# VectorE's drains replaced by a semaphore of its own, in a two-layer graph kernel on one core

## The chip, the cores and the metric

The kernel runs on one core of a Trainium2 chip. The metric is the time that the device needs for one execution, in microseconds. Before the change it is 2659.04 us, the median of three runs (2654.21 to 2662.23). The engines are TensorE (PE in the profile; PEld is its weight load), VectorE (DVE), ScalarE (ACT), GpSimd (POOL) and SyncE (SP). A "q" behind the name (DVEq, SPq) is that engine's own queue of instructions that occupy no datapath, such as a drain or the issue of a DMA.

## The reference, cut to what matters

Two layers over one graph of 8192 nodes with 128 features each. `adj` is an 8192x8192 matrix of zeros and ones in float32 (256 MB), thin except in its first rows.

```python
# layer 0: attention over the neighbours
h = relu(layernorm(x));  H = h @ W.T + b;  s = H @ a_s;  r = H @ a_r
e = leaky_relu(A * s + A * r.T);  att = softmax(where(A > 0, e, NEG), axis=1)
x = x + att @ H
# layer 1: sum over the neighbours, then the maximum over them
h = relu(layernorm(x)) @ weight
out = relu(adj @ h + bias)
x = x + max over the neighbours j of row i of out[j]
```

## The kernel before

A tile is 128 rows of the graph, and there are 64. Tile 0, with the densest rows (the hubs), is handled by separate code. The work has these stages.

**Stream (about 0 to 1150 us).** `load_tile(n)` on SP brings 4 MB of `adj` into one of two buffers. It waits until PE has packed tile n-2. PE's `pack(n)` (L1037) folds eight columns into one word, and `number_words(n)` (L1046) adds the word's number; it writes to one of two halves of PSUM. VectorE's `extract(n)` (L1358 to L1402) then turns the 1024 words of each row into a list of neighbours: it takes the eight largest (MAX8), strikes them out (MATCH_REPLACE8, which the profile shows as a MATCH_VALUE_LOAD and the replacement), and so on; it unpacks the bits and repeats the game over the found nodes. Each of these operations reads what the one before wrote, and a `dve.drain()` stands between every two. Tiles come in four groups, and the denser tiles (1 to 11, steps 16 to 26) take more rounds.

**Ranking and attention (about 230 to 1400 us, inside the stream).** When the last tile of a group is extracted, `classify` and `rank_rows` on VectorE sort its rows by degree. POOL scatters the records (L670) once the rank is there (L1456), and from then on handles ranked tiles q: `gather_h` (L684) fetches one row of H per neighbour slot and partition with an indirect DMA into a ring of 64 slots. ScalarE forms raw scores (L833, L834), VectorE's `scores(q)` (L1468, L1470) makes their maximum, ScalarE exponentiates (L842) and scales the gathered rows (L850), PE sums them (L1093, L1094), VectorE's `close(q)` (L1492, L1494) divides, ScalarE normalizes, PE multiplies with the second weight, and POOL scatters the row into `y_table` (L694). In which step n of the stream each q has its turn stands in a written table (`STEP`); every engine runs its program strictly in that order, so a wait of one q holds back the tiles behind it on the same engine.

**Dense rows of layer 1 (about 1400 to 1800 us).** VectorE unpacks bits (L1567) and PE multiplies them (L1210). POOL gathers the rows of the thin tiles (L717), and VectorE adds them up in `sum_rows` (L1485, L1625 to L1630).

**Maximum over the neighbours (1800 us to the end).** POOL gathers rows of `p_table` for 66 tiles in turn (L758). It may be four tiles ahead of VectorE's `best_of(n)` (L1485, L1715) and waits for room in the ring. `best_of` reduces a tile's slots with max; before it, `hot_tile(n)` (L1764) builds one-hot columns with which PE turns the rows back into their order (L1231). Between the tiles up to n = 35 VectorE also picks the neighbours of the hub rows out of `adj`: 60 times `hub_round` (L1668, L1671) and 48 times `hub_pick` (L1678, L1681). `hub_work` spreads them in proportion to POOL's slots.

**Order on VectorE.** A wait that a program states before an operation rides on that operation; where two are stated, the first becomes a small instruction of its own. A `then_inc` rides on the operation, or on a drain where it is written on the drain. In the kernel before nearly every signal that VectorE gives to another engine is written on a drain.

Of the kernel before, what the change touches and what calls it, by code (L numbers as in the profile page):

```python
# [9 lines left out]
P = 128  # L10
N = 8192
D = 128
T = N // P
# [222 lines left out]
def build(nc, x, adj, W0, b0, a_s, a_r, W1, b1, out):  # L236
    ctx = ExitStack()
    with ctx:
# [6 lines left out]
        def sem(name):  # L245
# [202 lines left out]
        s_unpacked, s_bits, s_bitsfree, s_relu, s_ptr, s_prow = (  # L448
            sem(n) for n in ("s_unpacked", "s_bits", "s_bitsfree", "s_relu", "s_ptr", "s_prow"))
# [25 lines left out]
        def _(sp):  # L475
# [84 lines left out]
            for c in range(DENSE_BATCHES):  # L560
                if c + 2 < DENSE_BATCHES:
                    sp.wait_ge(s_unpacked, c + 1)
# [705 lines left out]
        def _(dve):  # L1268
            dve.memset(eps_col[:], EPS)
# [61 lines left out]
            def statistics(n):  # L1331
                for j in range(8):
                    dve.bn_stats(stats[:, j, :], xs[:, 8 * n + j, :])
                dve.drain()
                for j in range(8):
                    dve.bn_aggr(mv[:, 8 * n + j, :], stats[:, j, :])
                dve.drain().then_inc(s_var, 1)

            def shifts(n):
                cols = slice(8 * n, 8 * n + 8)  # L1340
                dve.wait_ge(s_scale, n + 1)
                dve.scalar_tensor_tensor(shift[:, cols], mv[:, cols, 0], -1.0, rstd[:, cols], ALU.mult, ALU.mult)
                dve.drain().then_inc(s_rstd, 1)
# [14 lines left out]
            def extract(n):  # L1358
# [18 lines left out]
                dve.tensor_scalar(words_i[:, 0:taken], words[:, 0:taken], VSCALE, None, ALU.mult)  # L1377
                dve.drain()
# [3 lines left out]
                                  bit_mask[:].unsqueeze(1).to_broadcast(wide), ALU.bitwise_and)  # L1382
                dve.drain()
                dve.tensor_tensor(node[:, 0:taken, :], words_no[:, 0:taken].unsqueeze(2).to_broadcast(wide),
                                  bit_node[:].unsqueeze(1).to_broadcast(wide), ALU.add)
                dve.drain()
                flat = node[:, 0:taken, :].rearrange("p a b -> p (a b)")
                dve.scalar_tensor_tensor(flat, bits[:, 0:taken, :].rearrange("p a b -> p (a b)"), 0.0, flat,
                                         ALU.is_gt, ALU.mult, accum_out=with_own[:, t:t + 1])
                dve.drain()  # L1390
                dve.scalar_tensor_tensor(flat, flat, label[:, t:t + 1], flat, ALU.not_equal, ALU.mult,
                                         accum_out=without[:, t:t + 1])
                dve.drain()
                dve.max(found[:, 0:8], flat)
                dve.drain()
                for r in range(8, w, 8):
                    dve.match_replace(flat, found[:, r - 8:r], flat, 0.0)
                    dve.drain()
                    dve.max(found[:, r:r + 8], flat)
                    dve.drain()  # L1400
# [3 lines left out]
            def classify(g):  # L1404
# [6 lines left out]
                dve.tensor_scalar(held, rec[g][:, :, lists], 0.0, None, ALU.is_gt)  # L1411
                dve.drain()
                dve.tensor_reduce(degree[:, cols], held, AX.X, ALU.add)
                dve.tensor_copy(rec_u[g][:, :, lists], rec[g][:, :, lists])
                dve.drain()
                dve.tensor_scalar(row_class[:, 0:n], degree[:, cols], float(m - 1), None, ALU.min)
                dve.tensor_tensor(own[:, cols], with_own[:, cols], without[:, cols], ALU.subtract)
                dve.drain()
                dve.tensor_tensor(one_hot[:, 0:m * n].rearrange("p (c t) -> p c t", t=n),
                                  row_class[:, 0:n].unsqueeze(1).to_broadcast([P, m, n]),  # L1420
                                  class_no[:, max(CLASSES) - m:max(CLASSES)].unsqueeze(2).to_broadcast([P, m, n]), ALU.is_equal)
                dve.drain().then_inc(s_onehot, 1)
# [425 lines left out]
```

## Time and profile before

| | us |
|---|---|
| median of three runs | 2659.04 |
| lowest and highest | 2654.21, 2662.23 |
| profiled execution, its own time | 2658.55 |
| span of its records | 2656.8 |
| PE busy | 1292.3 (49%) |
| DVE busy | 1519.5 (57%) |
| ACT busy | 465.0 (18%) |
| POOL busy | 1422.1 (54%) |

Busy time counts operations on the datapath; a drain is not in it. An engine's idle time is split by what ended it. "Issue" is time in which the engine waited for nothing that the profile shows, neither a semaphore nor an operation before it. "Remote" and "another core or an unknown queue" are waits whose releaser the records do not name. The granted clock of TensorE was 0.725 of full speed on average.

### The profile page before, as it was taken

The page shows a single profiled execution, that of the slowest core. Times are in us where ns is not written, and L with a number is a line of the kernel's source. Part 1 is how long each engine was busy: PE and PEld are TensorE (multiplying, and loading weights), DVE is VectorE, ACT ScalarE, POOL GpSimd, SP SyncE. Part 2 cuts the span into 40 slices and gives each one's busy share as a digit, 9 for nine tenths or more (in the row PEclk, how much of TensorE's full clock was granted, in tenths as well). Part 3 has the DMA queues.
Part 4 walks back from the last instruction along what each step waited for, and adds up shares of the span by engine and source line. Part 5 has one row for each costly group of instructions (what it writes and reads, how often), then busy time and mean ns, then how long its engine had stood idle before and what let it go on. Part 6 is the DMA issues. An engine that isn't in the chain of part 4 may idle for free.

```text
span 2656.8 us, 20293 instructions
## 1 busy us (share of the span) xinstructions
PE 1292.3 (49%) x5093; PEld 670.8 (25%) x5093; DVE 1519.5 (57%) x3498; ACT 465.0 (18%) x1561; POOL 1422.1 (54%) x1465
## 2 busy tenths in 40 slices
PE   3765145636153645533445997862442212475036
PEld 1432023313032312323441443320111100132013
DVE  6888757866442625436244654454658755893234
ACT  1541134502122402443450000000000000000000
POOL 0002655461746463567535556366757775567763
PEclk8887668777676866765676998885676555687568
DMA  9999857787773879852343223114112321212221
GB/s 343 398 372 410 266 164 281 283 278 295 265 288 107 329 249 380 343 180 66 81 132 81 71 63 80 30 48 89 51 45 67 91 75 36 53 50 52 71 69 44
DMA packets 161767, 443.50 MB, mean 167 GB/s; under 512 B 31986, under 2 KB 90661, under 8 KB 128750
## 3 DMA queue, kind: packets, MB, share of 16 engines
q1 hardware_dynamic: 78974, 307.90, 30.4%
q0 software_dynamic: 49360, 108.63, 15.9%
q10 hardware_dynamic: 33312, 25.63, 3.2%
q8 instruction: 43, 0.70, 0.1%
q14 instruction: 78, 0.64, 0.1%
HBM read 404.00 MB, written 37.98 MB: 166 GB/s over the span
## 4 chain that ended last, share of the span: by engine, by line
DVE 20%; PE 17%; another core or an unknown queue 17%; issue 16%; DVEq 11%; POOL 10%; SPq 3%; DMA 3%; ACT 2%; ACTq 0%; POOLq 0%
PE psV L1210 10%; POOL ring L758 6%; POOL rec_all L758 4%; DVE words L1375 2%; DVEq L1374 2%; PE psV L1037 2%; DMA a_buf<-in_adj 2%; DVE words L1366 2%; DVE words L1370 2%; DVEq L1369 2%; PE psH L1093 2%; SPq L479 2%; PE psV L1231 1%; DVEq L1486 1%
## 5 line engine op out<-in xcount | busy, mean ns | idle before, releaser
L684 POOL DMA_INDIRECT ring<-h_table,srec x505 | 496.1, 982 | 292.6 <-issue 150.0
L1037 PE MATMUL psV<-a_buf,bit_ident 128*128 128x512 bf16 x1024 | 326.7, 486 | 219.7 <-DMA a_buf<-in_adj 148.2
L758 POOL DMA_INDIRECT rec_all<-p_table,srec x325 | 320.6, 986 | 190.7 <-issue 97.8
L1231 PE MATMUL psV<-a_buf,trec 128*128 128x512 f32 (+1 forms) x398 | 237.3, 751 | 256.3 <-DVEq L1717 102.6
L1093 PE MATMUL psH<-ring,ident 128*128 128x128 f32 x1010 | 159.3, 320 | 149.5 <-remote 60.6
L1037 PEld LDWEIGHTS psV<-a_buf,bit_ident 128*128 128x128 bf16 x1024 | 117.5, 117 | 410.9 <-issue 305.2
L1210 PE MATMUL psV<-rec_all,a_buf 128*128 128x512 bf16 x888 | 205.6, 388 | 26.8 <-issue 26.2
L717 POOL DMA_INDIRECT ring<-y_table,srec x191 | 185.0, 968 | 60.8 <-issue 60.2
L1231 PEld LDWEIGHTS psV<-a_buf,trec 128*128 128x128 f32 x398 | 95.5, 248 | 394.7 <-issue 186.6
L1093 PEld LDWEIGHTS psH<-ring,ident 128*128 128x128 f32 x1010 | 152.3, 234 | 160.5 <-issue 146.9
L1231 PE MATMUL psH<-a_buf,trec 128*128 128x512 f32 x124 | 79.6, 776 | 211.3 <-DVEq L1486 139.5
L758 POOL DMA_INDIRECT ring<-p_table,srec x154 | 150.4, 976 | 49.8 <-issue 46.3
L694 POOL DMA_INDIRECT y_table<-trec,srec x63 | 64.5, 1023 | 169.8 <-ACT trec L886 142.3
L1764 DVE TENSOR_SCALAR a_buf<-a_buf,bits 128x1024 f32<-128x1024 f32 (+1 forms) x146 | 97.6, 702 | 92.7 <-remote 46.6
L1567 DVE TENSOR_SCALAR rec_all<-a_buf 128x512 uint16<-128x512 uint16 x296 | 68.1, 300 | 117.8 <-remote 67.3
L850 ACT ACTIVATE ring<-ring,prob 128x128 f32<-128x128 f32 x423 | 128.9, 388 | 5.4 <-issue 3.9
L1210 PE MATMUL psV<-wbuf,a_buf 128*128 128x512 bf16 x456 | 113.9, 402 | 32.1 <-issue 27.4
L1210 PEld LDWEIGHTS psV<-rec_all,a_buf 128*128 128x128 bf16 x888 | 87.8, 99 | 140.0 <-issue 40.9
L1121 PE MATMUL psT<-w_sb,hT 128*128 128x128 f32 x126 | 35.6, 411 | 172.6 <-ACT hT L875 145.5
L1366 DVE MAX8 words<-psV 128x8 f32<-128x1024 f32 x63 | 77.7, 1233 | 57.5 <-remote 43.8
L1002 ACT ACTIVATE hn<-psV 128x512 f32<-128x512 f32 (+1 forms) x12 | 7.0, 588 | 580.0 <-issue 281.0
L670 POOL DMA_INDIRECT records<-rec_all,rank x63 | 61.1, 970 | 87.6 <-DVEq L1456 69.3
(259 smaller groups left out, 2299.6 us busy)
## 6 DMA issues: line engine op xcount, KB each, us to landing
a_buf<-in_adj SPq DMA_DIRECT2D x256, 1024.0 KB
ring<-h_table,srec POOLq DMA_INDIRECT x505
trec<-records ACTq DMA_DIRECT2D x63, 128.0 KB
packed<-wbuf ACTq DMA_DIRECT2D x28, 256.0 KB
a_buf<-packed SPq DMA_DIRECT2D x7, 1024.0 KB
rec_all<-p_table,srec POOLq DMA_INDIRECT x325
h_table<-stage POOLq DMA_DIRECT2D x16, 258.0 KB, 8.1
a_buf<-r_row SPq DMA_DIRECT2D x1, 4096.0 KB
```

The source lines that it names most:

```text
L684: pool.indirect_dma_start(ring[:, A_AT[q] + j, :], None, h_table, bass.IndirectOffsetOnAxis(srec_u[g][:, i, LIST + j:LIST + j + 1], 0)).th ...
L694: pool.indirect_dma_start(y_table, bass.IndirectOffsetOnAxis(srec_u[g][:, i, ROW1:ROW1 + 1], 0), trec[:, q % RECORDS, :], None).then_inc(s ...
L717: pool.indirect_dma_start(ring[:, Y_AT[m] + j, 0:D], None, y_table.rearrange("n (two d) -> (n two) d", two=2), bass.IndirectOffsetOnAxis(s ...
L758: pool.indirect_dma_start(ring[:, at + j, 0:D] if at < RING else side[:, at - RING + j, :], None, p_table, bass.IndirectOffsetOnAxis(slot, ...
L850: act.activation(row, row, ACT.Copy, scale=prob[q % 2][:, j:j + 1])
L1037: last = pe.matmul(psV[n % 2][:, h * BANK:(h + 1) * BANK].rearrange("p (g n) -> p g n", n=P), bit_ident[:, k, :], rows[:, :, k, :], start= ...
L1093: pe.matmul(psH[q % 2][:, 0:D], ident[:], ring[:, A_AT[q] + j, 0:D], start=(j == 0), stop=False)
L1210: last = pe.matmul(psA[c % 2], y_part[part][:, at:at + D], bit_rows[(c * BLOCKS + i) % 3][:, k, :], start=(i == 0 and k == 0 and part == 0 ...
L1231: pe.matmul(psO[b % len(psO)][:, 0:width], results[:, n % RESULTS, :], hot[:, c % HOT, at:at + width], start=(ranked_tile(n) == FIRST[g]), ...
L1366: dve.max(words[:, 0:8], src)
L1567: last = dve.tensor_scalar(bit_rows[n % 3][:, k, :].bitcast(U16).rearrange("p (u n) -> p u n", n=P), words_in[c % 2][:, :, b * P:(b + 1) * ...
L1764: dve.tensor_scalar(hot[:, c % HOT, 0:width], hub_iota[:, 0:width], hot_row[:, hot_column(g, i, j):hot_column(g, i, j) + 1], None, ALU.is_ ...
```

## The change

The program gets a semaphore `s_own` that VectorE alone signals and waits for. Where an operation needs the result of the one before, the drain between them goes; the first operation signals `s_own`, and the second waits for the running count. Where a drain carried a signal for another engine, the signal now rides on the operation. Drains that only separated independent work are left out, and where a scratch tile is used again, a wait on the semaphore that the last user had signalled is stated (`s_att` in `close`, `s_ysum` in `sum_rows`, `s_max` in `best_of`). `s_unpacked` goes; SP waits for `s_bits` in its place. The set-up code, the hub's dense scores and the slow path keep their drains.

```diff
+            own_steps = itertools.count(1)
...
-                dve.max(words[:, 0:8], src)
-                dve.drain()
+                dve.max(words[:, 0:8], src).then_inc(s_own, 1)
+                dve.wait_ge(s_own, next(own_steps))
                 dve.match_replace(V[:], words[:, 0:8], src, 0.0).then_inc(s_drained, 1)
-                dve.drain()
-                dve.max(words[:, 8:16], V[:])
-                dve.drain()
+                dve.wait_ge(s_drained, n + 1)
+                dve.max(words[:, 8:16], V[:]).then_inc(s_own, 1)
+                dve.wait_ge(s_own, next(own_steps))
                 for r in range(16, taken, 8):
-                    dve.match_replace(V[:], words[:, r - 8:r], V[:], 0.0)
-                    dve.drain()
-                    dve.max(words[:, r:r + 8], V[:])
-                    dve.drain()
+                    dve.match_replace(V[:], words[:, r - 8:r], V[:], 0.0).then_inc(s_own, 1)
+                    dve.wait_ge(s_own, next(own_steps))
+                    dve.max(words[:, r:r + 8], V[:]).then_inc(s_own, 1)
+                    dve.wait_ge(s_own, next(own_steps))
...
-                dve.scalar_tensor_tensor(e, e, ALPHA, e, ALU.mult, ALU.max)
-                dve.drain()
-                dve.reduce_max(m_neg[q % 2][:], e, axis=AX.X, negate=True)
-                dve.drain().then_inc(s_e, 1)
+                dve.scalar_tensor_tensor(e, e, ALPHA, e, ALU.mult, ALU.max).then_inc(s_own, 1)
+                dve.wait_ge(s_own, next(own_steps))
+                dve.reduce_max(m_neg[q % 2][:], e, axis=AX.X, negate=True).then_inc(s_e, 1)
...
                 dve.wait_ge(s_summed, q + 1)
-                dve.reciprocal(l_inv[:], l_sum[:, c:c + 1])
-                dve.drain()
+                if q > 0:
+                    dve.wait_ge(s_att, q)
+                dve.reciprocal(l_inv[:], l_sum[:, c:c + 1]).then_inc(s_own, 1)
+                dve.wait_ge(s_own, next(own_steps))
                 dve.scalar_tensor_tensor(row, psH[q % 2][:, 0:D], l_inv[:, 0:1], row, ALU.mult, ALU.add,
-                                         accum_out=x_sum[:, c:c + 1])
-                dve.drain().then_inc(s_att, 1)
+                                         accum_out=x_sum[:, c:c + 1]).then_inc(s_att, 1)
...
-                dve.max(best, hub_list)
-                dve.drain()
+                dve.max(best, hub_list).then_inc(s_own, 1)
+                dve.wait_ge(s_own, next(own_steps))
                 if n < HUB_KEEP // 8 - 1:
-                    dve.match_replace(hub_list, best, hub_list, 0.0)
-                    dve.drain()
+                    dve.match_replace(hub_list, best, hub_list, 0.0).then_inc(s_own, 1)
+                    dve.wait_ge(s_own, next(own_steps))
...
+                    dve.wait_ge(s_max, n)
+                    over_slots(row, at, k, ALU.max).then_inc(s_own, 1)
+                    dve.wait_ge(s_own, next(own_steps))
...
                 else:
-                    over_slots(result, at, k, ALU.max)
-                    dve.sem_inc(s_max, 1)
+                    over_slots(result, at, k, ALU.max).then_inc(s_max, 1)
```

The same pattern is applied in `statistics`, `shifts`, the rest of `extract`, `classify`, `rank_rows`, `scale_rows`, `split_y`, `sum_rows`, `hub_round`, `join_top`, `final` and `hub_close`.

## Rows read from the trace of the kernel before

**Rows 1.** Chain that ended last, share of the span by engine.

```profile
DVE 20%; PE 17%; another core or an unknown queue 17%; issue 16%; DVEq 11%; POOL 10%; SPq 3%; DMA 3%; ACT 2%; ACTq 0%; POOLq 0%
```

**Rows 2.** Windows: length; busy us (operations) of PE, PEld, DVE, ACT, POOL; clock; DMA share; GB/s.

```profile
0.00:227.00 227.00, 127.98 (x640) 69.14 (x640) 184.46 (x599) 81.87 (x209) 15.78 (x32) 0.87 0.99 374
...
316.00:370.00 54.00, 9.40 (x54) 7.94 (x55) 20.15 (x44) 9.08 (x28) 34.22 (x36) 0.56 0.48 148
...
1455.00:1800.00 345.00, 287.96 (x1280) 127.23 (x1278) 177.56 (x575) 9.00 (x14) 183.66 (x189) 0.90 0.21 57
...
2109.00:2270.00 161.00, 35.18 (x46) 13.80 (x46) 83.12 (x118) 0.00 (x0) 103.98 (x109) 0.56 0.22 59
2270.00:2376.00 106.00, 61.24 (x108) 24.93 (x109) 96.75 (x185) 1.69 (x3) 59.16 (x60) 0.76 0.20 53
```

**Rows 3.** VectorE in order of time, a round of the hub's picks; idle before in brackets.

```profile
2215.99 0.66 DVE L1678 MAX8 a_buf<-a_buf 128x8 f32<-128x480 f32 x1 [2.08 <-issue]
...
2217.47 0.64 DVE L1681 MATCH_REPLACE8 a_buf<-a_buf 128x480 f32<-128x480 f32 x1
2220.19 0.66 DVE L1678 MAX8 a_buf<-a_buf 128x8 f32<-128x480 f32 x1 [2.08 <-issue]
```

**Rows 4.** Window from a POOL run's start to VectorE's first late instruction.

```profile
541.20:563.30 22.10, 12.73 (x40) 4.74 (x40) 18.68 (x43) 0.90 (x4) 16.91 (x18) 0.77 1.02 401
```

**Rows 5.** VectorE in order of time, steps 14 and 15: start us, duration us.

```profile
222.51 0.18 DVE L1379 TENSOR_SCALAR words_no<-words_i 128x24 int32<-128x24 int32 x1
222.60 0.35 DVE L1381 TENSOR_TENSOR bits<-words_i,bit_mask 128x192 int32<-128x192 int32 x1
...
225.85 0.34 DVE L1397 MATCH_REPLACE8 node<-rec_all,node 128x192 f32<-128x192 f32 x1
226.27 0.36 DVE L1399 MAX8 rec_all<-node 128x8 f32<-128x192 f32 x1
226.70 1.23 DVE L1366 MAX8 words<-psV 128x8 f32<-128x1024 f32 x1
```

**Rows 6.** ScalarE in order of time, an operation that waits for the one before.

```profile
411.32 0.29 ACT L867 ACTIVATE t_log<-t_var,eps_col 128x1 f32<-128x1 f32 x1
411.64 0.20 ACT L870 ACTIVATE t_rstd<-t_log 128x1 f32<-128x1 f32 x1
```

**Rows 7.** In order of time: signals from VectorE to ScalarE, from ScalarE to VectorE.

```profile
1015.09 0.17 DVE L1470 TENSOR_REDUCE m_neg<-e_sc 128x1 f32<-128x15 f32 x1
...
1015.32 0.31 ACT L842 ACTIVATE prob<-e_sc,m_neg 128x15 f32<-128x15 f32 x1 [50.37 <-DVEq L1471]
...
1282.36 0.28 ACT L834 ACTIVATE e_sc<-srec 128x1 f32<-128x1 f32 x1
...
1282.74 0.17 DVE L1468 SCALAR_TENSOR_TENSOR e_sc<-e_sc 128x7 f32<-128x7 f32 x1 [11.18 <-issue]
```

**Rows 8.** In order of time, three places: what PE delivers, VectorE's operation on it.

```profile
220.86 0.61 PE L1046 MATMUL psV<-word_no,ones_bf 128*128 128x512 bf16 x2 [1.12 <-ACT wbuf L807]
...
365.51 0.37 PE L1094 MATMUL psH<-trec,ident 128*128 128x128 f32 x1 [1.73 <-issue]
...
370.33 0.16 DVE L1492 RECIPROCAL l_inv<-l_sum 128x1 f32<-128x1 f32 x1
...
608.33 0.59 PE L1046 MATMUL psV<-word_no,ones_bf 128*128 128x512 bf16 x2
...
617.40 1.23 DVE L1366 MAX8 words<-psV 128x8 f32<-128x1024 f32 x1
```

**Rows 9.** POOL's waits from 1955 to 2376: us in total, times, longest.

```profile
POOL rec_all L758 <- DVEq L1486: 45.4, 6, 14.3
...
POOL rec_all L758 <- DVEq L1717: 24.6, 8, 5.6
```

**Rows 10.** In order of time: a pack of PE, and the load behind it on SP.

```profile
821.04 5.81 PE L1037 MATMUL psV<-a_buf,bit_ident 128*128 128x512 bf16 x16
...
852.41 0.80 SPq L479 DMA_DIRECT2D a_buf<-in_adj  x2
```

More of the change, by code:

```diff
@@ L1 @@
+import itertools
 from contextlib import ExitStack
@@ L447, in build @@
         s_wordsin = [sem(f"s_wordsin{i}") for i in range(2)]
-        s_unpacked, s_bits, s_bitsfree, s_relu, s_ptr, s_prow = (
-            sem(n) for n in ("s_unpacked", "s_bits", "s_bitsfree", "s_relu", "s_ptr", "s_prow"))
+        s_own, s_bits, s_bitsfree, s_relu, s_ptr, s_prow = (
+            sem(n) for n in ("s_own", "s_bits", "s_bitsfree", "s_relu", "s_ptr", "s_prow"))
         s_pst = [sem(f"s_pst{i}") for i in range(2)]
@@ L561, in _ @@
                 if c + 2 < DENSE_BATCHES:
-                    sp.wait_ge(s_unpacked, c + 1)
+                    sp.wait_ge(s_bits, (c + 1) * BLOCKS)
                     load_words(c + 2)
@@ L1332, in statistics @@
                 for j in range(8):
[L1333 to L1334 removed]
+                    last = dve.bn_stats(stats[:, j, :], xs[:, 8 * n + j, :])
+                last.then_inc(s_own, 1)
+                dve.wait_ge(s_own, next(own_steps))
                 for j in range(8):
[L1336 to L1337 removed]
+                    last = dve.bn_aggr(mv[:, 8 * n + j, :], stats[:, j, :])
+                last.then_inc(s_var, 1)
             def shifts(n):
@@ L1341, in shifts @@
                 dve.wait_ge(s_scale, n + 1)
-                dve.scalar_tensor_tensor(shift[:, cols], mv[:, cols, 0], -1.0, rstd[:, cols], ALU.mult, ALU.mult)
-                dve.drain().then_inc(s_rstd, 1)
+                dve.scalar_tensor_tensor(shift[:, cols], mv[:, cols, 0], -1.0, rstd[:, cols], ALU.mult, ALU.mult).then_inc(s_rstd, 1)
             def mean_column():
@@ L1391, in extract @@
+                dve.wait_ge(s_own, next(own_steps))
                 dve.scalar_tensor_tensor(flat, flat, label[:, t:t + 1], flat, ALU.not_equal, ALU.mult,
[L1392 to L1400, printed above, removed]
+                                         accum_out=without[:, t:t + 1]).then_inc(s_own, 1)
@@ L1401, in extract @@
+                dve.wait_ge(s_own, next(own_steps))
+                for r in range(0, w, 8):
+                    if r > 0:
+                        dve.match_replace(flat, found[:, r - 8:r], flat, 0.0).then_inc(s_own, 1)
+                        dve.wait_ge(s_own, next(own_steps))
+                    last = dve.max(found[:, r:r + 8], flat)
+                    if r + 8 < w:
+                        last.then_inc(s_own, 1)
+                        dve.wait_ge(s_own, next(own_steps))
                 if w < GROUPS[g][2]:
@@ L1546, in split_y @@
                                for j in range(3))
-                dve.tensor_copy(hi, product)
-                dve.drain()
-                dve.tensor_tensor(rest, product, hi, ALU.subtract)
-                dve.drain()
-                dve.tensor_copy(mid, rest)
-                dve.drain()
-                dve.tensor_tensor(lo, rest, mid, ALU.subtract)
-                dve.drain().then_inc(s_split, 1)
+                dve.tensor_copy(hi, product).then_inc(s_own, 1)
+                dve.wait_ge(s_own, next(own_steps))
+                dve.tensor_tensor(rest, product, hi, ALU.subtract).then_inc(s_own, 1)
+                dve.wait_ge(s_own, next(own_steps))
+                dve.tensor_copy(mid, rest).then_inc(s_own, 1)
+                dve.wait_ge(s_own, next(own_steps))
+                dve.tensor_tensor(lo, rest, mid, ALU.subtract).then_inc(s_split, 1)
             dve.wait_ge(s_xin, 16)
```

147 lines of the change are left out of this document (71 added, 76 removed).

## The prediction

> **What bounds the kernel now.** I read the chain of waits first. VectorE and its drains hold 31% of it (20 and 11), PE 17, plain issue 16 and POOL 10 [rows 1]. A drain lies over the operation that it waits for, so the 11% is mostly running operations and not the drains' price. No engine bounds the kernel from end to end, so I cut the span into stages and asked for the busy time of each engine in each [rows 2].
>
> - 0 to 227 us: VectorE works 184 of 227 us, but the DMA engines are busy for 0.99 of the time. The stream of tiles is the limit, and VectorE trails it by a few us.
> - 227 to about 620 us: the dense tiles come. VectorE sets the pace, except where PE or a load arrives late.
> - 620 to 1455 us: a chain through POOL, ScalarE, PE and VectorE; no single engine holds it.
> - 1455 to 1800 us: PE works 288 of 345 us at a clock of 0.90. It is the bound.
> - 1800 us to the end: POOL's indirect DMAs, one each 1.25 us, until VectorE falls behind (2109 to 2376 us), and POOL again after that.
>
> There is a second thing in the windows. In 316 to 370 us VectorE has done only 20 us of work, PE 9, and the busy rows between 2109 and 2270 look alike [rows 2]. In order of time one sees why: a pick of the hub list begins each 4.20 us, with 2.08 us of "issue" before the MAX8, although nothing is missing [rows 3]. Its operations last 0.66 + 0.09 + 0.64 us, and with the gaps below a round takes 1.53 us undisturbed. Starts there sit on a grid of about 0.7 us, one instruction to a place, drains included. I call this starvation. It comes when POOL has issued indirect DMAs without a pause for 20 us or more, and it ends some us after POOL pauses. From the start of one such run VectorE did 43 operations in 22 us before its first late one [rows 4]; three other runs look the same (41 to 42 operations), and two longer runs held off until 62 and 106. That looks like a stock of instructions fetched ahead and not refilled. Drains take places in that stock.
>
> **The drain's price.** With a drain between, L1399 begins 0.08 us after L1397's end, and L1366 0.07 after L1399's [rows 5]. Over all undisturbed pairs it is 72 to 76 ns, I take 74. Two operations with nothing between overlap: L1381 starts 0.09 us before L1379 ends [rows 5]; that is the floor. The trace has no VectorE operation that waits for VectorE's own signal. The nearest row is ScalarE, which does just that: L870 starts 0.03 us after L867's end (31 to 32 ns in all such pairs) [rows 6]. PE's signals reach VectorE in 37 ns. The far bound is ScalarE to VectorE, 0.10 us, where the first of two waits is an instruction of its own [rows 7]. I take 33 ns, because the one-wait form is what the change writes, so a replaced drain gives 41 ns. By the bounds it gives between 160 and -29 ns.
>
> The count comes from the code and the counts of its lines: 63 extractions with 11 drains each and 238 more in their list rounds, 252 in scores and close, 217 in the hub's rounds and picks, and the rest smaller, 1840 in all. In VectorE's time that is 1840 x 0.041 = 75 us. What lies on the path:
>
> 1. To 227 us: 250 drains, 10.3 us. But tile 15 is ready at 220.86 + 0.61 = 221.5 us, and VectorE starts on it at 226.70 [rows 5, 8]. More than 5.2 us can't come. 5.
> 2. 227 to 316: 101 drains, 4.1.
> 3. 316 to 370: starved. VectorE could be 25 us sooner, but its L1492 waits for PE's L1094, which ends at 365.9 in starvation of its own; L1492 starts at 370.33 [rows 8]. 4.5.
> 4. 370 to 513: 195 drains, 8.0. POOL's records of group 1 wait for the rank at its end.
> 5. 513 to 617: 116 drains and starvation again. Tile 34 is ready at 608.9, VectorE takes it at 617.40 [rows 8]. The load behind it sits on SP, which starves too. 8.5.
> 6. 617 to 906: 226 drains, 9.3, half on the path, and 3 for the starved scores at 700 us: 7.6.
> 7. 906 to 1206: 271 drains, 11.1, half: 5.5.
> 8. 1206 to 1455: 142 drains, 5.8, half: 2.9.
> 9. 1455 to 1800: 159 drains beside PE's matmuls: 0. If PE were faster they would cost 6.
> 10. 1800 to 2109 and from 2376: 190 drains behind POOL's run: 0.
> 11. 2109 to 2376: POOL has 109 + 60 DMAs there, 169 x 1.25 = 211 us, in 267. VectorE has 83 + 97 = 180 us of work and about 10 of gaps [rows 2]. Freed from drains, starvation hardly slows it: a round of picks is two instructions, 1.4 us of grid, against 1.5 us of work. So the stage shrinks towards POOL's 211, by at most 56. POOL's waits on VectorE say the same: 45.4 + 24.6 + 3.4 (a smaller row) us, of which the longest, 14.3, stems from PE [rows 9], leaves 59. I take 45, as the two engines are close and wait for each other.
>
> Sum: 5 + 4.1 + 4.5 + 8 + 8.5 + 7.6 + 5.5 + 2.9 + 45 = 91.
>
> Added waits: `close`, `sum_rows` and `best_of` state one wait more, 63 + 35 + 38 times. It makes the first wait an instruction, 0.065 us where VectorE stood waiting; behind it are the tile's extraction and POOL. With 26 such waits in `close` and some 15 in the others that is 2.7 us. Signals to other engines: L842 on ScalarE starts 0.06 us after L1470's end with the drain's signal [rows 7]; riding on the operation it should be 0.03. With some 80 handovers on the path, 2.5 us. These cancel. SP's wait for `s_bits` is met at the same moment as before, and the loads behind it are needed 40 us later: 0. The dropped drains at the ends of `extract` and `scores` may let the next operation overlap, up to 5 us more; I leave it in the range.
>
> 2658.55 - 91 = 2567.5 in the profiled execution's time. That execution lies 0.5 us below the median of the runs, so I predict **2568 us**.
>
> What speaks against it: the trace has undrained pairs overlapping by 90 ns and drained ones 74 apart [rows 5], so a drain is not free here. The Trainium skill says (VectorE: DVE Perf Modes, "The DRAIN you can't avoid") that the pipeline empties after every operation whether or not a semaphore follows, and that one should cut operations rather than semaphores. By that rule a semaphore in a drain's place still finds the pipe to be emptied, and the sum would be near 0. The overlap in the rows speaks against it for independent operations; for dependent ones no row decides.
>
> **The rivals.**
>
> - *Gaps shrink, starvation stays.* If the late instructions come from POOL's traffic whatever VectorE asks for, and VectorE's ride on the grid is no shorter, items 3, 5 and 11 fall back to 41 ns per drain (28, 116 and 162 drains: 1.1, 4.8, 6.6). The sum is 40, the time 2618. For it: PE starves without any drain (L1094, 1.73 us of issue) [rows 8]. Against it: in [rows 3] each drain takes places of its own.
> - *SP starves longer.* A faster VectorE joins POOL's runs together, and SP issues loads only when they end: the load behind the pack that ended at 826.9 was issued at 852.41, 25 us late [rows 10]. Then the 46 us of items 1 to 8 are given back and 45 stay: 2614.
> - *No change.* An own signal returns as late as a drain does, 74 ns, and starvation stays: 2658.
> - *Slower.* The own wait is answered at 102 ns, as in [rows 7]: +29 ns. It decides from the point where the answer takes over 74 ns. On the path are 250 + 101 + 28 + 195 + 116 + half of 639 + 162 = 1172 drains, so +34: 2693. For it: L1468 behind ScalarE takes it. Against it: the 0.1 us has a separate wait instruction in it, and PE's signals take 37 ns.
>
> **How the numbers follow.** Forecast 0.50, starvation stays 0.22, SP starves 0.15, no change 0.05, slower 0.08. Within 0.3% (8 us) is about what a measurement of this kernel can't tell from no change. The first three are faster: 0.87; same 0.05; slower 0.08. The forecast's own range goes from 2505 (59 us in item 11, a second 59 in the starved scores, overlaps and halves of items 6 to 8, and 35 in items 1 to 5) to 2600. With the second and third it reaches to 2640, and about 0.15 is left out.
>
> **What would show it.** VectorE's dependent pairs 30 to 40 ns apart instead of 74, and L842 30 ns after L1470. Busy time of VectorE near 1520 us as before. Hub picks in the last stage a round each 1.5 us, POOL's waits on VectorE after 1955 us below 20, and the run of L758 nearly unbroken. PE's stage from 1455 to 1800 as long as before. L1492 at 365 us and tile 34 at 609 minus the shift, not earlier. Wrong would be: gaps of 70 or more; or gaps of 33 with the picks still 4.2 us apart; or SP's tile loads issued later behind their packs than now.

## The result, and the profile after the change

| | before | after |
|---|---|---|
| median of four runs, us | 2656.62 | 2612.91 |
| lowest and highest | 2649.83, 2662.23 | 2606.38, 2614.08 |
| profiled execution, its own time | 2658.55 | 2613.49 |
| span of its records | 2656.8 | 2611.7 |

The ratio is 0.9837, with a 95% interval of 0.9813 to 0.986. The kernel is faster by 43.7 us, less than half of the 91 that were forecast. The busy times of the engines stayed within 6 us of what they were, except that of VectorE, which fell by 24 us from 1519.5 (columns: busy us and share of the span, instructions):

```profile
PE 1286.9 (49%) x5093; PEld 672.1 (26%) x5093; DVE 1495.5 (57%) x3498; ACT 464.7 (18%) x1561; POOL 1420.8 (54%) x1465
```

The chain of the changed kernel answers to [rows 1]. VectorE's queue, where the drains stood, fell from 11% to nothing. What replaced it is not VectorE's work, whose share fell too: the releasers without a name, PE, the DMAs, ScalarE and SP's queue grew.

```profile
another core or an unknown queue 21%; PE 20%; DVE 16%; issue 14%; POOL 11%; DMA 7%; ACT 6%; SPq 5%; ACTq 0%; DVEq 0%; POOLq 0%
```

VectorE in order of time in the changed kernel, undisturbed, at the place of [rows 5] and in the same columns. A dependent operation starts 0.03 us after the one before it; it was 0.07 to 0.08.

```profile
221.19 0.09 DVE L1376 MATCH_VALUE_LOAD V<-words,V 128x8 f32 x1
221.27 1.21 DVE L1376 MATCH_REPLACE8 V<-words,V 128x1024 f32<-128x1024 f32 x1
222.51 1.23 DVE L1378 MAX8 words<-V 128x8 f32<-128x1024 f32 x1
223.78 0.18 DVE L1380 TENSOR_SCALAR words_i<-words 128x24 int32<-128x24 f32 x1
```

Over all of VectorE's waits for itself the median gap is 35 ns, against 73 with a drain. So a replaced drain gives 38 ns (41 were forecast). The signals ride as forecast too: L843 on ScalarE starts 34 ns after L1472 ends, where [rows 7] had 60.

Now the same kernel in the last stage, a round of hub picks, which answers to [rows 3]. In brackets is the idle time before, and what ended it.

```profile
2173.18 0.64 DVE L1680 MATCH_REPLACE8 a_buf<-a_buf 128x480 f32<-128x480 f32 x1
2175.90 0.66 DVE L1677 MAX8 a_buf<-a_buf 128x8 f32<-128x480 f32 x1 [2.08 <-issue]
2177.30 0.09 DVE L1680 MATCH_VALUE_LOAD a_buf<-a_buf 128x8 f32 x1 [0.74 <-DVE a_buf L1677]
2177.38 0.64 DVE L1680 MATCH_REPLACE8 a_buf<-a_buf 128x480 f32<-128x480 f32 x1
2179.41 0.66 DVE L1677 MAX8 a_buf<-a_buf 128x8 f32<-128x480 f32 x1 [1.38 <-DVE a_buf L1680]
2181.50 0.09 DVE L1680 MATCH_VALUE_LOAD a_buf<-a_buf 128x8 f32 x1 [1.43 <-DVE a_buf L1677]
```

The drains are gone and a round still takes 3.5 to 4.2 us here, about as before (over the ten late rounds of each trace that follow one another the mean is 3.98 us before and 4.46 after). The releaser is now named: it is VectorE's own operation, which had ended 0.7 to 2 us earlier. Its signal comes late. Not every instruction of VectorE is late, only one that waits. Thirteen operations of the same stretch, in six rows (xN is how many a row joins):

```profile
2096.11 1.12 DVE L1734 SCALAR_TENSOR_TENSOR hT<-a_buf,shift,psT 128x128 f32<-128x128 f32 x4 [1.52 <-DVE V L1670]
2101.01 1.14 DVE L1741 SCALAR_TENSOR_TENSOR hT<-hT,log_var,a_buf 128x128 f32<-128x128 f32 x4 [3.78 <-remote]
2102.06 1.21 DVE L1764 TENSOR_SCALAR a_buf<-a_buf,bits 128x1024 f32<-128x1024 f32 x2
2103.20 3.35 DVE L1485 TENSOR_REDUCE trec<-rec_all 128x128 f32<-128x1920 f32 x1
2106.48 1.21 DVE L1667 MAX8 a_buf<-V 128x8 f32<-128x1024 f32 x1
2112.91 0.09 DVE L1670 MATCH_VALUE_LOAD V<-a_buf,V 128x8 f32 x1 [5.22 <-remote]
```

From 2101.01 eight operations follow each other without a gap, since none waits for VectorE. The next one needs the MAX8's result and starts 5.22 us late. Between 2070 and 2186 us none of 49 operations without such a wait is late, and 26 of 34 with one are, by 0.3 us or more. The late starts keep a pace: from one to the next pass about 1.4 us for every operation between them, however short it is. Over the 45 such pairs between 2069 and 2233 us the mean is 1.38 us, and it is 1.4 or 2.1 us where one operation lies between, mostly 2.8 with two, 3.5 to 5.6 with three, 8.4 with six and 11.2 to 11.9 with eight. A round of picks has three operations (MAX8, MATCH_VALUE_LOAD, MATCH_REPLACE8), and three times 1.4 is the 4.2 of [rows 3], where a round had two drains as well, and they took nothing extra.

The stretch with its windows, which answer to the last two of [rows 2] (same columns); all of it lies 39 us earlier and little is shorter:

```profile
2070.00:2233.00 163.00, 33.32 (x46) 13.16 (x46) 82.03 (x118) 0.00 (x0) 104.17 (x108) 0.55 0.23 59
2233.00:2332.00 99.00, 59.92 (x109) 24.44 (x110) 96.08 (x187) 1.68 (x3) 59.02 (x61) 0.81 0.23 57
```

POOL's waits for VectorE from 1917 to 2332 us, which answer to [rows 9] (us in total, times, longest), are the same as before but for 3 us:

```profile
POOL rec_all L759 <- DVE trec L1485: 46.1, 6, 13.6
...
POOL rec_all L759 <- DVE trec L1715: 21.2, 9, 4.6
```

PE, in the stretch of [rows 8], ends its sum at 356.60 + 0.37 us, and VectorE's L1493, which waits for it, starts at 365.30, 5.0 us earlier than before. Tile 34 is taken at 600.49, 16.9 us earlier:

```profile
356.60 0.37 PE L1095 MATMUL psH<-trec,ident 128*128 128x128 f32 x1 [2.42 <-issue]
```

```profile
365.30 0.16 DVE L1493 RECIPROCAL l_inv<-l_sum 128x1 f32<-128x1 f32 x1 [1.53 <-remote]
```

Where the 45 us of the two profiled executions arise, by events that both traces have (us; "forecast" is the sum of the prediction's items up to there):

| event | before | after | lead | forecast |
|---|---|---|---|---|
| VectorE takes tile 16 | 246.6 | 239.9 | 6.7 | 5 |
| VectorE takes tile 19 | 325.0 | 314.7 | 10.3 | 9 |
| VectorE's first close | 370.3 | 365.3 | 5.0 | 13.6 |
| VectorE takes tile 34 | 617.4 | 600.5 | 16.9 | 30.1 |
| records of group 2 on POOL | 906.1 | 881.3 | 24.8 | 37.7 |
| POOL's first gather of the run at 1200 | 1199.9 | 1172.0 | 27.9 | 43.2 |
| first gather for the maximum | 1813.5 | 1775.4 | 38.1 | 46.1 |
| tile 16 of the last stage | 1989.8 | 1951.1 | 38.7 | 46.1 |
| tile 40 of the last stage | 2376.2 | 2331.5 | 44.7 | 91 |
| end | 2656.8 | 2611.7 | 45.1 | 91 |

### The profile page after: what moved, and what is told of

It reads as the page before. It is cut to its first block, busy times and chain, and to the rows that moved or that the text cites. A ratio compares the mean times of both kernels' runs of the same rounds, so it can differ in the third digit from the quotient of the medians.

```text
span 2611.7 us, 18582 instructions
## 1 busy us (share of the span) xinstructions
PE 1286.9 (49%) x5093; PEld 672.1 (26%) x5093; DVE 1495.5 (57%) x3498; ACT 464.7 (18%) x1561; POOL 1420.8 (54%) x1465
## 4 chain that ended last, share of the span: by engine, by line
another core or an unknown queue 21%; PE 20%; DVE 16%; issue 14%; POOL 11%; DMA 7%; ACT 6%; SPq 5%; ACTq 0%; DVEq 0%; POOLq 0%
PE psV L1211 10%; DMA a_buf<-in_adj 6%; POOL ring L759 6%; POOL rec_all L759 5%; PE psV L1038 3%; SPq L480 2%; PE psH L1094 2%; ACT ring L851 2%; SPq L493 2%; PE psV L1232 2%; DVE a_buf L1677 2%; DVE a_buf L1680 1%; DVE trec L1485 1%; DVE V L1670 1%
## 5 line engine op out<-in xcount | busy, mean ns | idle before, releaser
L685 POOL DMA_INDIRECT ring<-h_table,srec x505 | 493.9, 978 | 280.7 <-issue 150.9
L1038 PE MATMUL psV<-a_buf,bit_ident 128*128 128x512 bf16 x1024 | 320.7, 479 | 215.5 <-DMA a_buf<-in_adj 155.2
L1211 PE MATMUL psV<-rec_all,a_buf 128*128 128x512 bf16 x888 | 212.0, 393 | 51.1 <-issue 50.6
L1094 PE MATMUL psH<-ring,ident 128*128 128x128 f32 x1010 | 162.6, 324 | 142.6 <-issue 100.6
L1094 PEld LDWEIGHTS psH<-ring,ident 128*128 128x128 f32 x1010 | 154.4, 237 | 155.0 <-issue 145.3
L1211 PE MATMUL psV<-wbuf,a_buf 128*128 128x512 bf16 x456 | 105.0, 388 | 3.8 <-issue 3.1
```

The costliest lines, as they stand in the source:

```text
L685: pool.indirect_dma_start(ring[:, A_AT[q] + j, :], None, h_table, bass.IndirectOffsetOnAxis(srec_u[g][:, i, LIST + j:LIST + j + 1], 0)).th ...
L1038: last = pe.matmul(psV[n % 2][:, h * BANK:(h + 1) * BANK].rearrange("p (g n) -> p g n", n=P), bit_ident[:, k, :], rows[:, :, k, :], start= ...
L1094: pe.matmul(psH[q % 2][:, 0:D], ident[:], ring[:, A_AT[q] + j, 0:D], start=(j == 0), stop=False)
L1211: last = pe.matmul(psA[c % 2], y_part[part][:, at:at + D], bit_rows[(c * BLOCKS + i) % 3][:, k, :], start=(i == 0 and k == 0 and part == 0 ...
```

## The experiments

The runs were made on six occasions, each with runs of the kernel before beside them. On three of them the kernel before takes 2657, 2668 and 2667 us, on the other three 2284, 2284 and 2285 us. For five of the six the number of the chip is known: on chip 10 the kernel before took 2668 us beside e1 to e4 and 2284 beside e13 to e15, so it is not the chip alone that decides. So times are compared only within an occasion, and I call the occasions slow-signal and clean; why follows from the traces below.

**On a slow-signal occasion (kernel before 2668.32 us): e1_hub_drained, e3_pool_pauses, e4_extract_only, e2_no_strike_out.** In e1 the hub's rounds and picks have their drains again.

```diff
-                dve.max(best, hub_list).then_inc(s_own, 1)
-                dve.wait_ge(s_own, next(own_steps))
+                dve.max(best, hub_list)
+                dve.drain()
```

> The changed kernel with the drains put back inside the hub's rounds and picks (some 215 of the 1840), and nowhere else. Theory R (results come late): in the starved stretches an operation's result reaches VectorE's next wait about 1.4 us per operation late, whether that wait is a drain or a semaphore, so drains cost no place there. Then a pick in the starved stretch stays at 4.0 to 4.2 us, and only the undisturbed rounds lose 0.04 us per drain: 2613 to 2619 us. Theory P (the prediction's: every instruction takes a place of the supply, drains too): a pick goes back from three places to five, the stretch of 163 us grows by some 35: about 2648.

2631.78 us, ratio 0.984 (0.9795 to 0.9885): nothing lost against the changed kernel's 0.9837, within some 12 us; the 35 us more of theory P would be seen. VectorE in order of time, with drains, in the late stretch of e1:

```profile
2193.93 0.66 DVE L1677 MAX8 a_buf<-a_buf 128x8 f32<-128x480 f32 x1 [2.43 <-issue]
...
2197.78 0.66 DVE L1677 MAX8 a_buf<-a_buf 128x8 f32<-128x480 f32 x1 [2.08 <-issue]
...
2201.98 0.66 DVE L1677 MAX8 a_buf<-a_buf 128x8 f32<-128x480 f32 x1 [2.08 <-issue]
```

3.9 and 4.2 us from one pick to the next: three operations and two drains take as long as three operations with semaphores. Over its ten late rounds the mean is 4.67 us, against 4.46 in the changed kernel. Drains take no places; theory P, the prediction's, falls. Outside the late stretch a pick takes 1.53 us in e1 and in the kernel before, and 1.45 in the changed one.

In e3 POOL is made to pause.

```diff
-                if n >= BUFS:
+                if n in (18, 20, 22, 24, 26):
+                    pool.wait_ge(s_max, n)
+                elif n >= BUFS:
```

> The changed kernel, but before tiles 18, 20, 22, 24 and 26 of the last stage POOL waits until VectorE has reduced every earlier tile (it was up to four ahead), which breaks its run of 184 DMAs into pieces of 30 to 55 us with pauses of 5 us and more. If the starvation needs a long unbroken run of POOL's DMAs, VectorE's late operations between 2070 and 2233 us (81 us of lateness) mostly go, and VectorE, which sets this stage, gains 15 to 35 us: 2578 to 2598. If it comes with the traffic and not with the run's length, VectorE stays late and the pauses come on top: 2618 to 2632.

2628.94 us, ratio 0.9842 (0.9811 to 0.9874). The gain did not come: the ratio is that of the changed kernel, and the loss of 5 to 19 us that was the other expectation isn't excluded by the interval, but not shown. The trace shows both effects at once. VectorE's late starts begin at 2239 us instead of 2070, 280 us after the start of POOL's gathers for tile 16 and not 118, and their lateness sums to 35 us instead of 81. (Its waits between 2188 and 2228 us are not late: each ends within 0.3 us of the landing of POOL's gather.) During the first five pieces, of 19 to 55 DMAs each, VectorE has no late start, and the late ones come 37 us after the last pause; counted from tile 16, tile 24 comes 28 us later than in the changed kernel (214.8 against 187.1 us), and tile 47 still 10 us later (420.6 against 411.0). Pauses put the lateness off but did not pay.

In e4 only `extract` has the new form (931 drains).

> The kernel before, with the own semaphore in extract's operations alone (931 of the 1840 drains). Theory: the gain of the changed kernel before 1150 us (29 us by VectorE's start of the last extraction) comes from extract in about its share of the drains on the path there, some 20 to 25 us, and nothing follows after: 2632 to 2637 against 2657 of before. Rival: the other half (signals that ride, scores, close) carries as much, then extract alone gives 15 or less: 2642 or more.

2648.19 us, ratio 0.9921 (0.9894 to 0.9947), so 21 us less than before (14 to 28), as expected: extraction carries half of the gain.

e2 was to make the picks shorter by leaving the MATCH_REPLACE8 out.

> The changed kernel with the MATCH_REPLACE8 of each hub pick left out, so that the picks are no longer the right ones; a pick is one MAX8. Both R and P say that VectorE's operations set the stage of 1917 to 2332 us: in its starved part a pick falls from 4.0 to about 1.4 us, after it from 1.45 to 0.7. With 29 picks starved or half starved and 18 after, VectorE is 75 us and more faster and POOL's waits for it (69 us) become the limit: 55 to 65 us less, 2550 to 2560. Rival: the stage waits for PE's turning of the rows (hot columns) and not for the picks: less than 15 us gained, 2598 or more.

303704.58 us: without it every kept list looks full, and the program takes its slow path for dense graphs. The run says nothing on the question; e6 asks it again.

**On a clean occasion (kernel before 2283.58 us): e5 to e8.** e5 is the changed kernel.

> The changed kernel once more, as the yardstick of this chip for the other three. Expected: its ratio to the kernel before again 0.981 to 0.986, some 43 us less than the kernel before on the same chip, and in its trace the same stretches in which VectorE's results come late (about 305 to 365, 655 to 718 and 2070 to 2233 us).

2266.64 us, ratio 0.9922 (0.9904 to 0.994). Neither the ratio nor the late stretches came. The kernel before is 385 us faster than on the first of the occasions above, and e5's POOL and VectorE are as long busy as ever (1423.4 and 1498.6 us). PE's busy time is 52 us shorter (1235.3 against 1286.9, at a granted clock of 0.77 and not 0.73), which is far from 385. A round of picks in the trace of e5:

```profile
1928.37 0.66 DVE L1677 MAX8 a_buf<-a_buf 128x8 f32<-128x480 f32 x1
1929.07 0.09 DVE L1680 MATCH_VALUE_LOAD a_buf<-a_buf 128x8 f32 x1
1929.14 0.64 DVE L1680 MATCH_REPLACE8 a_buf<-a_buf 128x480 f32<-128x480 f32 x1
1929.82 0.66 DVE L1677 MAX8 a_buf<-a_buf 128x8 f32<-128x480 f32 x1
```

1.45 us for each, all through the stage, although POOL issues 570 DMAs there in one run without a pause. The traces record each semaphore's update. Matched with the operation that sends it (updates more than 25 us off left out), they give this table, worked out from the traces:

```
                          signals seen / over 0.3 us late / sum of these, us
                          VectorE            PE                 ScalarE
before, slow-signal       460 /  2 /   1.7   558 / 95 / 479.6   562 / 20 / 65.1
after, slow-signal       1387 / 96 / 173.7   521 / 93 / 481.5   559 / 19 / 56.0
before, clean (e14)       600 /  0 /   0     712 /  0 /   0     750 /  0 /   0
after, clean (e5)        1987 /  0 /   0     713 /  0 /   0     752 /  0 /   0
```

That is what divides the occasions: on the one no signal is late, on the other about one in six of PE's and one in fourteen of VectorE's. PE's numbers depend on the matching: if each update is given to the last operation of its semaphore that had ended, 130 and 136 are late instead of 95 and 93. The surest single case is one of 15.8 us (e10, below). (Before the change VectorE's lateness hides in drains, which carry few signals.) On the slow-signal occasions 22 to 30% of each engine's updates are also missing from the trace.

e6 leaves the MATCH_REPLACE8 of the picks out as e2 did, and keeps off the slow path.

```diff
-                    dve.match_replace(hub_list, best, hub_list, 0.0).then_inc(s_own, 1)
-                    dve.wait_ge(s_own, next(own_steps))
+                    pass
...
-                    dve.tensor_tensor(flags[:, 0:1], hub_step[:], hub_cap[:], ALU.is_gt)
+                    dve.tensor_tensor(flags[:, 0:1], hub_step[:], hub_cap[:], ALU.is_lt)
```

> The changed kernel with the MATCH_REPLACE8 of each hub pick left out and the comparison that would then choose the slow path turned round; a pick is one MAX8, and the picks are not the right ones. If VectorE's operations set the stage of 1917 to 2332 us (theories R and P alike), a pick in its late part falls from 4.0 to about 1.4 us, afterwards from 1.45 to 0.7, and POOL's 69 us of waits go: 50 to 65 us less than the changed kernel on the same chip. If the stage waits for PE's turning of the rows instead: less than 15 us.

2264.18 us, ratio 0.9916 (0.9899 to 0.9933): 2.5 us less than e5, no difference. Here VectorE does not set the stage. POOL does; of its waits in e5 from 1671 to 2051 us for VectorE 2.4 us are left (same columns as above):

```profile
POOL rec_all L759 <- DVE trec L1715: 1.8, 6, 0.3
POOL ring L759 <- DVE trec L1485: 0.3, 1, 0.3
POOL rec_all L759 <- DVE trec L1485: 0.3, 1, 0.3
```

e7 has a drain wherever VectorE waits for itself (1548 drains in its trace; before has 1922, after 82), and keeps all else of the change.

```diff
-                dve.max(words[:, 0:8], src).then_inc(s_own, 1)
-                dve.wait_ge(s_own, next(own_steps))
+                dve.max(words[:, 0:8], src)
+                dve.drain()
```

> The changed kernel with a drain at each place where it waits for s_own, s_drained or s_chunk in VectorE's own program; the signals to other engines still ride on the operations, the drains that only separated independent work stay out, and the added waits stay. It parts the change in two. Theory: of some 43 us, the semaphore in a drain's place brings 30 to 40 and the rest 5 to 13, so this kernel is 5 to 13 us faster than the kernel before. Rival: the signals that ride (some 120 drains on handovers) bring half or more: 20 us or more faster than before.

2274.16 us, ratio 0.9959 (0.9944 to 0.9973). The 374 drains that went with signals or separated nothing bring 9.4 us (6 to 13), as expected in size, the 1466 that became semaphores 7.5, where 30 to 40 of 43 were expected.

e8 spreads the hub's work (`C_SLOTS[1:HUB_AT - 10]` becomes `C_SLOTS[1:HUB_AT - 4]` in `hub_work`).

> The changed kernel with the hub's work spread over six tiles more (up to tile 43 of the last stage instead of 37), where VectorE is idle for 28% of the time beside a busy PE. Where VectorE sets the stage (2070 to 2329 us) it has some 8% less to do: 5 to 12 us less than the changed kernel on the same chip. Rival: tiles 37 to 43 wait for PE, and VectorE's added work delays the hot columns that PE waits for, so nothing is gained: within 3 us.

2265.58 us, ratio 0.9924 (0.9904 to 0.9945): no change against e5, as POOL sets the stage.

**The same four on a slow-signal occasion (kernel before 2666.93 us): e9 to e12.**

> The changed kernel as the yardstick of a third chip. The two chips so far differ: on one the kernel before takes 2657 to 2668 us and VectorE's results come late in several stretches, on the other it takes 2284 and no result is late. Expected: with late results a ratio of 0.981 to 0.986, without them 0.990 to 0.994.

> The changed kernel with one MAX8 for each hub pick (no MATCH_REPLACE8; the picks are not the right ones). On a chip without late results it brought nothing (2.5 us), since POOL sets the last stage there. On a chip with them VectorE sets 2070 to 2329 us: 50 to 65 us less than the changed kernel on the same chip. If it is below 15 us there too, VectorE's operations are not what the stage waits for.

> The changed kernel with drains where it waits for its own semaphore; signals still ride. Without late results it took 9.4 us of the 17 that the whole change brings. With late results: the semaphore in a drain's place brings 25 to 35 of the 43 us, this kernel is 8 to 18 us faster than the kernel before. Rival: half or more comes from the signals that ride: 20 us or more.

> The changed kernel with the hub's work spread up to tile 43 of the last stage. Without late results it changed nothing (1 us), as POOL sets the stage. With late results: 5 to 12 us less than the changed kernel on the same chip; rival: within 3 us, because tiles 37 to 43 wait for PE.

- e9, the changed kernel: 2621.9 us, ratio 0.9851 (0.9812 to 0.989), as expected; VectorE late again from 2079 to 2243 us.
- e10, one operation in a pick: 2621.58 us, ratio 0.9834 (0.98 to 0.9868). Expected were 50 to 65 us less; nothing came.
- e11, drains back: 2644.91 us, ratio 0.9929 (0.9904 to 0.9954). Signals and dropped drains bring 22 us here (12 to 26), the semaphore in a drain's place 23. The median is the rival's, but the interval reaches into the 8 to 18 us that were expected.
- e12, picks spread later: 2631.22 us, ratio 0.9876 (0.9839 to 0.9913). No gain; the two intervals overlap, so a loss isn't shown either.

In e10 the late picks did become shorter: mostly 1.4 us each (0.7 to 3.2), so an operation that waits for the one before costs about 1.4 us whatever it does (same columns):

```profile
2193.75 0.66 DVE L1677 MAX8 a_buf<-a_buf 128x8 f32<-128x480 f32 x1 [2.55 <-remote]
2195.15 0.66 DVE L1677 MAX8 a_buf<-a_buf 128x8 f32<-128x480 f32 x1 [0.74 <-DVE a_buf L1677]
2196.55 1.37 DVE L1677 MAX8 a_buf<-a_buf 128x8 f32<-128x480 f32 x2 [0.74 <-DVE a_buf L1677]
```

POOL went from tile 27 to tile 30 in 35.8 us instead of 63.8 in e9, 28 gained. From tile 30 to 36 it took 86.4 instead of 65.4, and 21 were given back. The place is in PE's, VectorE's and ScalarE's rows of e10, in order of time:

```profile
2257.89 0.60 PE L1240 MATMUL psF<-ident,hn 128*128 128x128 f32 x4
...
2274.34 0.86 DVE L1733 SCALAR_TENSOR_TENSOR hT<-a_buf,shift,psT 128x128 f32<-128x128 f32 x3 [18.30 <-remote]
2274.34 0.49 ACT L1003 ACTIVATE hn<-psV 128x384 f32<-128x384 f32 x1 [42.89 <-remote]
```

PE's L1240 ends at 2258.48. The update of its semaphore stands at 2274.26 in the trace, 15.8 us later, and VectorE and ScalarE, which both wait for it, start at 2274.34. Most of what VectorE saves here is waited out at a signal of PE.

**On a clean occasion (kernel before 2284.10 us): e13, e14, e15.** In e13 the last stage gathers 66 slots instead of 560 (`for j in range(k)` becomes `range(1)` in `gather_p`, with the counts to match). e14 is the kernel before, e15 the changed one.

> The changed kernel, but in the last stage POOL gathers one slot of each of the 66 tiles instead of all 560, so the maximum there is over old rows. Theory: on a chip where signals come late they do so only while POOL issues DMAs without a pause; here no such run is left after about 1765 us, so VectorE's and PE's late signals end there, and VectorE's own work (some 380 us busy) takes tiles 0 to 47 through in 400 to 450 us instead of 587, the last 19 tiles in 60 to 100 instead of 220. Rival: the lateness has nothing to do with POOL; then VectorE's picks are again 4.2 us apart in some stretch. On a chip without late signals the run tells only how long VectorE and PE need by themselves.

> The kernel before, unchanged, to have its trace from the same chip as the next one. Expected on a chip with late signals 2650 to 2670 us, without them 2280 to 2290.

> The changed kernel on the same chip. With late signals: 35 to 50 us less than the kernel before, of it nothing between 280 and 370 us and 3 to 10 between 1955 and 2376. Without late signals: 14 to 20 us less, gained before POOL's last run begins and kept.

e13 took 2053.29 us (ratio 0.9, 0.8954 to 0.9045). With so few of POOL's DMAs tiles 0 to 47 take 417 us and the rest, to the end of the kernel, 114, against 523 and 220 in e5. The first was expected at 400 to 450, the second at 60 to 100. Whether late signals need POOL's run could not be seen, as none was late. e14 took 2283.8 us (1.0, 0.9985 to 1.0015) and e15 2265.69 (0.9928, 0.9897 to 0.9959). This pair of traces shows where the change gains when no signal is late: 1.5 us at POOL's first DMA, 8.3 at its 180th, 9.5 at the 420th, 14.8 at the first gather for the maximum (1540.4 against 1525.6), 14.5 at tile 57 and 15.6 at the end. The last stage gives next to nothing (0.8 us), for POOL hardly waits in it.

**Once more: e16 and e17 (kernel before 2285.09 us).** e17 gathers every second slot.

> One gathered slot for each of the 66 tiles of the last stage, on another occasion than e13, which met no late signals. If signals are late in the earlier stages here (the kernel before near 2660 us): theory, lateness needs POOL's DMAs one behind the other, so after 1800 us, where they are gone, no signal of VectorE or PE is more than 0.3 us late, and tiles 0 to 47 take about the 610 us that they took in e13. Rival: late signals after 1800 us too, and the tiles take longer than in e13 by 20 us or more.

> The changed kernel with half of the slots of each tile of the last stage gathered (287 of 560 DMAs), so the maximum is partly over old rows. POOL's own time there falls to about 370 us. If signals are late on this occasion: theory, POOL must pause for VectorE and its runs stay short, so lateness after 1800 us is gone or under a quarter of the changed kernel's. Rival: it stays above half.

2057.96 us (0.9007, 0.898 to 0.9033) and 2087.24 us (0.9135, 0.9108 to 0.9161), again on a clean occasion, so the question stays open. (The 610 us in the expectation of e16 was a miscount; the tiles took 417 in both.)

## Why the prediction was wrong

**The failed step is item 11**, 45 us in 2109 to 2376: "Freed from drains, starvation hardly slows it: a round of picks is two instructions, 1.4 us of grid". It gave 6.0 (lead 38.7 to 44.7). That is 39 of the 46 us by which the forecast of 91 was off. The pace of 4.2 us was read rightly [rows 3] and put down to the wrong thing. Drains take no places: the same pick takes 4.2 us with its drains (e1) and 3.5 to 4.2 without, and eight of VectorE's operations in a row run without a gap in the stretch if none waits for VectorE. What has a price is the operation, 1.4 us each, and a round has three and not two; e10, with one operation in a pick, has 1.4 us.

The profile before the change had the mark of it: each of VectorE's 20 late operations between 2109 and 2210 us starts within 0.15 us of the end of a drain, so it was the drain that ended late. In place of the places there are late signals. An operation's completion reaches whoever waits for it 0.7 to 5 us late, at the pace of 1.4 us for each operation since the last late start, and a semaphore is answered no earlier than a drain was. And where VectorE was freed in part, a late signal of PE stood next (e10). That some stock of another kind lies behind the pace is neither shown nor excluded: PE runs 40 matmuls without a gap and then starts one instruction each 1.4 us (rows at the end).

**The terms before it.** Items 1 and 2 hold (10.3 us at tile 19, 9 forecast). Item 3, +4.5, was -5. It read the wait wrongly: before the change VectorE was itself late up to a drain that ends at 370.24, and L1492 starts 0.09 us behind it without waiting for PE. After the change VectorE's operations keep their late pace, so that its lead is down to 6.4 us at the operation before the close (370.04 against 363.61), and the close then does wait, 1.5 us, for a sum of PE that had ended 8.3 us earlier. Why 5.0 is left, about the lead of POOL's run (5.3, its start at 280.6 against 275.3), is open. Items 4 and 5 gave 11.9 for 16.5. With item 3 that is why the lead at tile 34 was 16.9 and not 30. Item 6 holds (7.9, forecast 7.6). Item 7 gave 3.1 for 5.5. Item 8, up to the dense rows, gave some 10 for 2.9; no run tells why. Item 9 is right: from 1486 to 1753 us the lead of PE's matmuls stays at 37.5. Item 10 is right (0.6). The sum of items 1 to 10 was forecast at 46 and measured at 38.7, where items 3 to 5 and 7 fell short by 17 and item 8 made up 7, which is luck.

**The drain's price** of 41 ns was 38, in 1466 places. The Trainium skill (VectorE: DVE Perf Modes, "The DRAIN you can't avoid"), weighed against it, says that the pipeline empties after each operation and that a semaphore there costs nothing extra. It speaks of that emptying, not of a drain that the program writes, and for such a drain the sum near 0 that was drawn from it did not come: dependent pairs stand 35 ns apart with a semaphore and 73 with a written drain on every occasion.

**Signals and added waits** were to cancel, at 0. e7 and e11 say 9.4 and 22 us for the signals that ride and the drains dropped without a substitute. It is half of the gain, and I had half of it in the wrong account: item by item all 1840 drains were priced as replaced. Of these 374 were not replaced but left out, and there the next operation overlaps: 1732 of VectorE's operations start before the one before has ended, against 1502, and the overlaps sum to 118 us against 99. That is most of the 24 us by which its busy time fell. With drains back in the 1466 other places (e7) it is as low, 1500.9 us against 1524.5 of the kernel before on such an occasion (e14). The prediction named up to 5 us for it, kept that in the range, and expected the busy time to stay near 1520.

**The rivals.** "Gaps shrink, starvation stays" forecast 2618 and 40 us; by its own terms (items 3, 5 and 11 at 1.1, 4.8 and 6.6) the sum is 45.6 and the time 2613. The time (2612.91) and the picks, which keep their pace, are its own. That the sum fits to a microsecond is luck, since item 3 was 6 us below its term and item 8 some 7 above. Its reason, traffic of POOL, is not enough: 570 DMAs in a row on a clean occasion made nothing late. On a slow-signal occasion POOL's run does bear on it, as pauses in e3 put the lateness off by 161 us. "SP starves longer" forecast 2614. Its mark is there once: the load of [rows 10] is issued at 830.61, 34.5 us behind the end of its pack (790.91 + 5.24) instead of 25.5. But the lead at POOL's records behind it is 24.8, more than the 20.7 at tile 36, so no 46 us were given back. "No change" and "slower" fell with the 35 ns.

## What to carry to other kernels

A semaphore of its own in a drain's place is worth some 40 ns of VectorE's time for each pair, and drains that can go without a substitute were worth as much here in all with a quarter of the number, because the next operation then overlaps; count the two apart. Before an odd pace in a profile is priced, look which instructions are late: all of them, or only those that wait. If only those, a cheaper way of waiting does not help, and the next late signal stands behind the one that you remove. And measure a kernel on several occasions before reading 1% from it: the same code took 2284 and 2668 us on the chip with number 10.

## What the runs showed of the hardware that was not expected

- On some occasions, and not on others on the same chip, the engines' signals arrive late: none of 3452 on a clean one (e5), some 208 of 2467 on a slow-signal one, by 15.8 us in the surest case (e10), and the kernel takes 16 to 17% longer. The lateness sits in stretches, mostly beside long runs of POOL's indirect DMAs. Late starts lie multiples of 0.7 us apart, and from one to the next 1.4 us pass for each operation. A wait isn't always needed: PE's L1094 in the changed kernel waits for nothing between its matmuls, runs 40 of them without a gap and then one each 2.8 us, with a weight load 1.4 us behind each (at 344.00, 346.80 and 349.60):

```profile
335.75 6.67 PE L1094 MATMUL psH<-ring,ident 128*128 128x128 f32 x40
342.60 0.27 PE L1094 MATMUL psH<-ring,ident 128*128 128x128 f32 x1 [0.17 <-issue]
345.40 0.27 PE L1094 MATMUL psH<-ring,ident 128*128 128x128 f32 x1 [2.53 <-issue]
348.20 0.37 PE L1094 MATMUL psH<-ring,ident 128*128 128x128 f32 x1 [2.53 <-issue]
```

- Its cause is open. The Trainium skill (NOTIFIC — Programmer's Manual, "2.4 When the ring fills") says that a full queue of records, depending on how it is set, drops new ones, overwrites the oldest or holds up the engine that writes them. Records are missing on just these occasions (1387 of VectorE's signals seen against 1987), which would fit the first; that the recording holds up the engines is argued and not shown, since no run here is without it.
- POOL's indirect DMAs cost the same on both kinds of occasion: 983 ns on average for L685 in e5, 978 in the changed kernel's first profile.
